# Post-norm transformer layer with routed experts: who makes the low halves and the final sums behind the block loop, and at which tile the last batch's router steps stand

## The reference

```python
def reference(x, w_qkv, w_out, gate_w, gate_b, w1, b1, ..., ws3, bs3):
    x = layernorm(x + attention(x, w_qkv, w_out))         # 16 heads of 16, causal
    # feed-forward: 16 experts of width 176, 6 per token, and a shared one of width 352
    probs = softmax(x @ gate_w.T)
    _, idx = top_k(probs + gate_b, 6)
    for e in range(16):                                   # c is 0 where e was not chosen
        h = silu(x @ W1[e].T + B1[e]) * (x @ W3[e].T + B3[e])
        y += c[e] * (h @ W2[e].T + B2[e])
    z = (silu(x @ ws1.T + bs1) * (x @ ws3.T + bs3)) @ ws2.T + bs2
    return layernorm(x + y + z)
```

## Time and profile before

| what | us |
|---|---|
| three runs of the kernel | 1127.47, 1139.32, 1139.49 (median 1139.32) |
| the profiled execution, its own time | 1130.5 |
| its span, first to last instruction | 1128.7 |
| PE busy in it | 1036.1 (92%) |
| DVE, ACT, POOL busy | 748.7, 670.9, 740.6 |
| mean granted TensorE clock | 0.974 |

### The profile page before, as it was taken

How to read it: one execution, slowest core, us unless ns; L and a number is a source line. 1 busy time by engine, 2 the same in 40 slices (tenths; PEclk the granted TensorE clock), 3 DMA queues, 4 the chain that set the end, 5 groups by cost and what they waited for, 6 DMA issues and landing times.

```text
span 1128.7 us, 28318 instructions
## 1 busy us (share of the span) xinstructions
PE 1036.1 (92%) x8028; PEld 847.3 (75%) x8029; DVE 748.7 (66%) x2401; ACT 670.9 (59%) x1680; POOL 740.6 (66%) x676
## 2 busy tenths in 40 slices
PE   7899998989898998788998999999999999999991
PEld 4546464646464644387988999999999999999991
DVE  8786878786878787577765555555555555555455
ACT  3567676767676765665555555555555555555544
POOL 4224368787878888877635666666666666666665
PEclk9999999999999998899998999999999999999996
DMA  6624254545454535557867666677776666667593
GB/s 185 183 71 114 77 143 147 164 147 163 148 161 145 169 124 172 189 174 228 287 165 139 115 120 119 114 118 117 119 118 113 110 116 113 116 116 140 82 313 144
DMA packets 127037, 163.54 MB, mean 145 GB/s; under 512 B 18800, under 2 KB 107504, under 8 KB 126704
## 3 DMA queue, kind: packets, MB, share of 16 engines
q1 hardware_dynamic: 82240, 99.73, 31.6%
q0 software_dynamic: 39024, 54.29, 25.6%
q10 hardware_dynamic: 5696, 8.55, 2.4%
HBM read 65.36 MB, written 73.85 MB: 123 GB/s over the span
## 4 chain that ended last, share of the span: by engine, by line
PE 63%; DMA 12%; DVE 12%; issue 5%; ACT 4%; POOL 2%; SPq 1%; ACTq 0%; POOLq 0%; DVEq 0%
PE psum L1057 13%; PE psum L794 10%; PE psum L1084 10%; DMA z_d<-y_sb,tokens 9%; PE psum L836 5%; PE psum L824 4%; PE psum L809 4%; DVE rowmax L1496 3%; PE psum L1042 3%; PE psum L1068 3%; PE psum L1053 3%; PE psum L1023 2%; ACT probs L1160 2%; DMA stack_q<-shift_l 2%; PE psum L811 2%
## 5 line engine op out<-in xcount | busy, mean ns | idle before, releaser
L1160 ACT ACTIVATE probs<-psum 128x512 f32<-128x512 f32 (+2 forms) x384 | 186.5, 530 | 115.1 <-PE psum L824 113.2
L1496 DVE TENSOR_REDUCE rowmax<-psum 128x1 f32<-128x512 f32 (+3 forms) x352 | 211.7, 632 | 60.5 <-PE psum L811 58.7
L2029 POOL DMA_INDIRECT xs_d<-x1p,index x192 | 206.1, 1074 | 53.2 <-issue 40.3
L2103 POOL DMA_INDIRECT x_d<-y_sb,tokens x104 | 162.5, 1562 | 93.6 <-ACT y_sb L1354 65.7
L2103 POOL DMA_INDIRECT z_d<-y_sb,tokens x103 | 160.7, 1560 | 93.7 <-ACT y_sb L1354 51.1
L1835 DVE TENSOR_TENSOR xb_lo<-psum,xb_hi 128x256 fp32r<-128x256 f32 x207 | 87.7, 424 | 201.3 <-ACT xb_hi L1151 199.4
L1057 PE MATMUL psum<-we_hi_lo,xb_hi 128*128 x828 | 200.9, 324 | 0.0
L1354 ACT ACTIVATE y_sb<-psum,combine 128x256 f32<-128x256 f32 x207 | 98.3, 475 | 152.2 <-PE psum L1084 75.2
L1084 PE MATMUL psum<-we_hi_lo,hb_hi 88*128 (+1 forms) x828 | 175.2, 304 | 0.0
L809 PE MATMUL psum<-stack_k,stack_q 96*128 96x256 bf16 (+3 forms) x512 | 139.0, 311 | 9.2 <-DVE rowmax L1496 3.6
L1057 PEld LDWEIGHTS psum<-we_hi_lo,xb_hi 128*128 128x128 f32 x828 | 146.8, 190 | 0.0
(11 more groups left out here) (209 smaller groups left out, 2322.3 us busy)
## 6 DMA issues: line engine op xcount, KB each, us to landing
xb<-xs_d SPq DMA_DIRECT2D x207, 138.0 KB
stack_q<-q_h SPq DMA_DIRECT2D x48, 128.0 KB
stack_k<-k_h SPq DMA_DIRECT2D x45, 128.0 KB
w_raw<-in_we SPq DMA_DIRECT2D x9, 608.0 KB, 4.2
xT_raw<-in_xT SPq DMA_DIRECT2D x9, 512.0 KB, 4.2
stack_q<-q_m SPq DMA_DIRECT2D x32, 128.0 KB
stack_k<-k_m SPq DMA_DIRECT2D x32, 128.0 KB
x_res<-in_x SPq DMA_DIRECT2D x8, 512.0 KB, 3.7
```

The lines of the kernel that those rows point to most:

```text
L1160: nc.scalar.activation(probs[kt][:, heads[0]:heads[0] + n, :], st[f % ST_BANKS][:, 0:n * width].rearrange("p (h t) -> p h t", h=n), ACT.Ex ...
L1496: nc.vector.reduce_max(rowmax[gpar][:, heads[0]:heads[0] + n, qt], src, AX.X).then_inc(sm_free, 1)
L2029: nc.gpsimd.indirect_dma_start(out=xs_d[:, :], out_offset=bass.IndirectOffsetOnAxis(ap=index[tp][:, n:n + 1], axis=0), in_=x1p[tp][:, n // ...
L2103: nc.gpsimd.indirect_dma_start(out=(x1_d, z_d)[k % 2][:, :], out_offset=bass.IndirectOffsetOnAxis(ap=tokens[:, k:k + 1], axis=0), in_=y_sb ...
```

## The change

It has two parts.

**Behind the loop.** VectorE makes the low half of every tile to the last, GpSimd none. GpSimd sums `fin_x` and `fin_z` of all 16 units; it runs three units ahead of VectorE's statistics instead of two, and makes no low halves between. The units' statistics begin at tile 38 instead of 39. For units 10 to 15 VectorE adds the PSUM result in one step. ScalarE's `normalized` steps stand one tile earlier with them.

**Ahead of the loop.** The last batch's transposes stand at tile 7 (were 6), its router logits at 9 (8), softmax and choice at 10 (9), the store of its rows at 9 (8), its ranks at 12 (10), the table steps at 13, 14 and 16 (11, 12 and 14).

The rest (`bank_of`, `sum_of` with `SUM_BANKS`, `FINAL_ORDER` as plain order, the counts on `z_stored`) gives the same banks, order and counts as before: 16 units never reach the added wait `hc >= HC1 + SUM_BANKS`. TensorE has the same instructions; VectorE's list is five rows longer and GpSimd's fifteen rows shorter as printed with repeats merged.

```diff
-EPILOGUE_AT = {2: ("t0", "t1"), 4: ("p0", "p1"), 6: ("x0", "x1"), 8: ("r",), 10: ("d",)}
-NORMALIZE_TILE, SOFTMAX_TILE, STORE_X1_TILE, RANK_TILE = 5, 9, 8, 10
+EPILOGUE_AT = {2: ("t0", "t1"), 4: ("p0", "p1"), 7: ("x0", "x1"), 9: ("r",), 12: ("d",)}
+NORMALIZE_TILE, SOFTMAX_TILE, STORE_X1_TILE, RANK_TILE = 5, 10, 9, 12
...
-TABLE_TILES = (11, 12, 14)
+TABLE_TILES = (13, 14, 16)
...
-FINAL_FROM = DVE_LOW_UP_TO = T1 + 9
-SUMS_BY_POOL, NORMALIZED_BY_ACT = HC1 + 2, T_ALL // HT_TOK - 4
+FINAL_FROM, SUMS_AHEAD = T1 + 8, 3
+NORMALIZED_BY_ACT = T_ALL // HT_TOK - 4
+FINAL_ORDER = tuple(range(T_ALL // HT_TOK))
...
         @block.vector
-            def final_add(i):
+            def final_add(m):
 
+                i = FINAL_ORDER[m]
                 dve.wait_ge(down_done, ST * (i + 1))
-                y = sum_of(i).rearrange("p (q d) -> p q d", q=HALF)
-                if i < SUMS_BY_POOL:
-                    dve.wait_ge(fin_sum, i + 1)
-                    nc.vector.tensor_tensor(fin_x[i][:], y, fin_x[i][:], ALU.add).then_inc(z_done, 1)
-                else:
-                    dve.wait_ge(fin_loaded[i], 32)
-                    nc.vector.tensor_tensor(fin_z[i][:], y, fin_z[i][:], ALU.add).then_inc(fin_y, 1)
+                dve.wait_ge(fin_sum, m + 1)
+                nc.vector.tensor_tensor(fin_x[i][:], sum_of(i).rearrange("p (q d) -> p q d", q=HALF), fin_x[i][:],
+                                        ALU.add).then_inc(z_done, 1)
...
             for T in range(T1 + 2, FINAL_FROM + HALVES):
                 if T < T_SH:
                     hide(T)
-                if T - 1 < DVE_LOW_UP_TO:
+                if T - 1 < T_SH:
                     low(T - 1)
...
         @block.gpsimd
-            for T in range(DVE_LOW_UP_TO, FINAL_FROM + HALVES):
-                i = T - FINAL_FROM
-                if i == 0:
-                    final_sum(0)
-                    final_sum(1)
-                if T < T_SH:
-                    low(T)
+            for m in range(SUMS_AHEAD):
+                final_sum(m)
+            for m in range(HALVES):
                 for k, (_, end) in enumerate(FINAL_GROUPS):
-                    if i == end:
+                    if m == end:
                         final_inverse(k)
-                if i + 2 < SUMS_BY_POOL:
-                    final_sum(i + 2)
+                if m + SUMS_AHEAD < HALVES:
+                    final_sum(m + SUMS_AHEAD)
             final_inverse(len(FINAL_GROUPS) - 1)
```

More of the change, by code:

```diff
@@ L516, in postln_layer @@
         TABLE_STEPS = 11
+        SUM_BANKS = 6
         RANKED = 3
@@ L769, in _ @@
                 sp.wait_ge(added[n], 16 * ((BLOCKS + 1 - n) // 2))
-                for i in range(FINAL_FIRST):
+                for i in FINAL_ORDER[:FINAL_FIRST]:
                     load_final(i, src, dst)
-            for i in range(FINAL_FIRST, HALVES):
+            for i in FINAL_ORDER[FINAL_FIRST:]:
                 load_final(i, x1_d, fin_x)
                 load_final(i, z_d, fin_z)
-            for i in range(HALVES):
-                store_final(i)
+            for m in range(HALVES):
+                store_final(m)
             sp.wait_ge(out_stored, 16 * HALVES)
@@ L1020, in shared_down @@
                     pe.wait_ge(z_done, hc - 1)
+                elif t == 0 and hc >= HC1 + SUM_BANKS:
+                    pe.wait_ge(z_done, hc - SUM_BANKS + 1)
                 for j in range(HALF):
@@ L1390, in blocks, with normalized @@
                         split_late_w(m, half)
-            def normalized(i):
-                act.wait_ge(fin_shift_done, [first <= i for first, _ in FINAL_GROUPS].count(True))
-                for q in range(HALF if i < NORMALIZED_BY_ACT else 1):
+            def normalized(m):
+                i = FINAL_ORDER[m]
+                act.wait_ge(fin_shift_done, [first <= m for first, _ in FINAL_GROUPS].count(True))
+                for q in range(HALF if m < NORMALIZED_BY_ACT else 1):
                     last = nc.scalar.activation(fin_x[i][:, q, :], fin_x[i][:, q, :], ACT.Identity,
-                                                bias=fin_shift[:, i, q:q + 1], scale=fin_rstd[:, i, q:q + 1])
+                                                bias=fin_shift[:, m, q:q + 1], scale=fin_rstd[:, m, q:q + 1])
                 last.then_inc(fin_done, 1)
@@ L1465, in _ @@
             high(T_SH - 1)
-            for i in range(T_SH - FINAL_FROM - NORMALIZED_BEHIND, HALVES):
-                normalized(i)
+            for m in range(T_SH - FINAL_FROM - NORMALIZED_BEHIND, HALVES):
+                normalized(m)
         @block.vector
@@ L1900, in final_stats, with final_aggregate, normalized_half @@
                 else:
-                    dve.wait_ge(fin_sum, i + 1)
+                    dve.wait_ge(fin_sum, m + 1)
                 for q in range(HALF):
-                    last = nc.vector.bn_stats(fin_stats[:, i, q, :], fin_x[i][:, q, :])
+                    last = nc.vector.bn_stats(fin_stats[:, m, q, :], fin_x[i][:, q, :])
                 last.then_inc(fin_stats_done, 1)
-            def normalized_half(i):
-                dve.wait_ge(fin_shift_done, [first <= i for first, _ in FINAL_GROUPS].count(True))
-                nc.vector.tensor_scalar(fin_x[i][:, 1, :], fin_x[i][:, 1, :], fin_rstd[:, i, 1:2], fin_shift[:, i, 1:2],
+            def final_aggregate(m):
+                dve.wait_ge(fin_stats_done, m + 1)
+                settle(dve, passed_dve)
+                for q in range(HALF):
+                    last = nc.vector.bn_aggr(fin_mv[:, m, q, :], fin_stats[:, m, q, :])
+                last.then_inc(fin_mv_done, 1)
+            def normalized_half(m):
+                i = FINAL_ORDER[m]
+                dve.wait_ge(fin_shift_done, [first <= m for first, _ in FINAL_GROUPS].count(True))
+                nc.vector.tensor_scalar(fin_x[i][:, 1, :], fin_x[i][:, 1, :], fin_rstd[:, m, 1:2], fin_shift[:, m, 1:2],
                                         ALU.mult, ALU.add).then_inc(fin_half_done, 1)
@@ L1951, in _ @@
                     low_x1(split_x1_of(T))
-                i = T - FINAL_FROM
-                if i >= HC1:
-                    final_add(i)
-                if i >= 1:
-                    final_aggregate(i - 1)
-                if i >= 0:
-                    final_stats(i)
+                m = T - FINAL_FROM
+                if m >= 0 and FINAL_ORDER[m] >= HC1:
+                    final_add(m)
+                if m >= 1:
+                    final_aggregate(m - 1)
+                if m >= 0:
+                    final_stats(m)
             final_aggregate(HALVES - 1)
-            for i in range(NORMALIZED_BY_ACT, HALVES):
-                normalized_half(i)
+            for m in range(NORMALIZED_BY_ACT, HALVES):
+                normalized_half(m)
         @block.gpsimd
```

46 lines of the change are left out of this document (17 added, 29 removed).

## The result

| what | before | changed |
|---|---|---|
| median of 20 runs each, us | 1134.45 (1126.17 to 1140.36) | 1123.29 (1117.81 to 1130.17) |
| ratio, 95% interval | | 0.9908 (0.9889 to 0.9928) |
| the profiled execution's own time | 1130.5 | 1117.81 |
| its span | 1128.7 | 1115.7 |

A forecast was written before the change was run, and what follows sets the result against it. TensorE bounds the loop; only its 10.5 us idle ahead and the 22.2 us after it ends were winnable. 8.7 behind plus 2.5 ahead make 11.2; 1134.9 (middle of four executions) - 11.2 = 1123.7 us, range 1112 to 1134.

The forecast's parts named there:

- the tail: Behind the loop: low halves moved to VectorE and sums to GpSimd were to give 8.7 us, bounds 2.9 and 10.4.
- the front: Ahead of the loop: the reordered last-batch steps were to give 2.5 us by tile 18, bounds nothing and 6.8.
- the low half is never late: Behind the loop: VectorE's turn of 1.6 to 2.2 us against TensorE's 2.19 us tile removes TensorE's 2.09 us wait.
- the rule that I had weighed and not used: Tail: two-SBUF-input VectorE work and GpSimd SBUF reads block fully, up to a whole 1.26 us sum; 0.2 was kept.
- The wait for sum 15: End of the tail: unit 15's sum stands behind the inverse of units 8 to 11; VectorE loses 1.3 us.
- Rival 1: Tail: nine low halves block behind sums, 5.8 us on TensorE, leaving 2.9 of 8.7; 1125.1 us; chance 0.12.
- The waits of 1.5 and 1.7: Ahead of the loop: new TensorE waits for low halves of tiles 9 and 10, about 1.5 and 1.7 us.
- the 0.8 at the transposes: Ahead of the loop, tile 7: down product waits 0.8 us for tile 5's low half; 1.53 goes, gain 0.6.
- The slow tile: Ahead of the loop: tile at TensorE's lower clock, 2.85 instead of 1.60 us, was to go, giving 1.25.
- I take them as caught up just before the loop: Loop entry: the last batch's 24 scatters, starting 3.2 us later, at 1.35 us each, cost nothing.
- Rival 4: Front: scatters become its end, 20 us late at the slow ones' pace; 1139.7 us; chance 0.03.
- rival 2: Front only moves its waits and gives nothing, the tail still 8.7; 1121.8, or 1126.2 at median level; chance 0.22.

The follow-up runs named there:

- experiment 10: Changed kernel with the units behind the loop one tile later (T1 + 9), on a slower chip; first up product behind the loop to span end 64.0 us.
- experiment 2: Kernel before with only the front's new tile numbers, everything behind the loop as before; ratio 0.9993 to before.
- experiment 7: Changed kernel with GpSimd's sums four units ahead instead of three; first up product behind the loop to span end 60.6 us.
- experiment 8: Changed kernel with GpSimd's sums cut to 8 of 512 columns; first up product behind the loop to span end 58.2 us.
- experiment 5: Changed kernel again, no edit; ratio 0.9923 to before, 1123.98 against 1133.34 us.
- experiment 4: Changed kernel with ranks at tile 11 instead of 12 and tables one tile earlier; ratio 0.9949 to before.
- experiment 6: Changed kernel with ranks at tile 11, tables one tile earlier, and the last weight split behind tile 26 instead of 24; ratio 0.9930, 1123.79 us.
- experiment 9: Changed kernel with ranks at tile 14, tables at 15, 16 and 18, on a slower chip (before: 1157.35); 1165.63 us.
- experiment 11: Changed kernel with ranks at 11, last weight split behind tile 26 and sums four units ahead, on a slower chip; ratio 0.9917 to before.
- experiment 12: Changed kernel with units one tile earlier still, sums four ahead, on a slower chip; first up product behind the loop to span end 61.1 us.

## Why the prediction came out

**The total.** The time (1123.7 for 1123.29) and the range held, and the parts behind them less well. By the stretch the tail gives 68.2 (mean of 67.7, 68.1, 68.7) less 61.0 (mean of six traces, 60.1 to 61.5) = 7.2 us for 8.7. By the first block's result (changed front 576.84, 577.90, 577.51, 578.04, 577.15; old front 576.68, 579.10, 578.26) the front gives 0.5 us for 2.5, which by the spread of these could be nothing. That is 7.7 of the 11.2 measured. The other 3.5 us stand in neither part; the loop, which I had put at nothing, is the stage that is left for them. So the agreement of the total to 0.4 us is luck: the tail was put 1.5 us too high, the front 2.0 too high, and 3.5 us that no step of mine has made up for both. What was not luck is the level: the middle of four executions, 1134.9, was the median of before within 0.5 us.

**The tail: mechanism right, 1.5 us too much.**
- TensorE's waits for GpSimd went, as predicted. That "the low half is never late" failed, since I kept the 0.2 us of the earlier trace rows as the price of a sum beside it. Measured excesses are 0.88, 0.29, 0.71 and 0.95 on four low halves and 1.09 on one of x1, 3.9 us in sum.
- This is the rule that I had weighed and not used (the Trainium skill, SBUF — State Buffer, "Who interferes with whom"): the trace agrees with it, two SBUF operands on VectorE against a GpSimd instruction in SBUF, with a block of up to 1.09 us of a sum's 1.26. The rows of before agreed with it too, and I misread them. The first sum and a low half of x1 there, taken alone:

```profile
1080.08 1.30 POOL L2113 TENSOR_TENSOR fin_x<-fin_x,fin_z 128x512 f32<-128x512 f32 x1 [5.84 <-DMA fin_x<-x_d]
...
1092.32 0.77 DVE L1489 TENSOR_TENSOR x1T<-x1T_late,x1T 128x512 fp32r<-128x512 f32 x1 [0.38 <-ACT x1T L1151]
```

The low half of 0.63 us in the earlier trace rows started at 1081.03, late in a sum that ended at 1081.38, and ended 0.28 us behind it: its 0.2 was not the price of a block but the short rest of the sum that it met. And the sum of 1.74 in the earlier trace rows started at 1092.50, inside the 0.77 us above, and ended 1.15 us behind their end at 1093.09, which is nearly a whole sum of 1.26: there it was GpSimd that stood.

- With the blocks the last low half is done 43.5 us into the stretch (1098.48 - 1054.96) where I had 41.3. TensorE ends 1.0 us earlier, not 3.4.
- The wait for sum 15 is 0.72, not 1.3, and gives 0.6 of it back: the last shift moved 7.0 us nearer, with 8 to 9 predicted. The six units at 1.39, the two short inverses and the 5.4 us at the end came out as worked out.
- Rival 1 had the right mechanism with too high a price: a whole sum on each of nine low halves, 5.8 us on TensorE; five instructions were hit by more than 0.1 us, and the changed kernel's stretch is 60.7 us where my steps gave 59.0 (1120.0 - 1061.0). The price is the rest of a sum, and only where one runs.
- Of the 7.2 us, 3 to 4 hang on the units' one tile (experiment 10, one trace) and the rest on the exchange of low halves and sums.

**The front: right until tile 18, wrong at the loop's entry.** The waits of 1.5 and 1.7 came as 1.36 and 1.76, the 0.8 at the transposes as 0.72, and tiles 17 and 18 stand 2.1 and 2.4 us earlier, with 2.2 and 2.5 predicted. The slow tile did not go: the lower clock followed the two new waits as it had followed the one old one. The step that failed is "I take them as caught up just before the loop". I had their start right (525.3, measured 525.9) and their pace nearly (1.35 us each, measured 1.40), had them end at 557.8 where they ended at 559.1, and did not add the landing of the last (3.8 us) and the load of the first rows behind it (2.6 us). 558.1 + 1.0 + 3.8 + 2.6 = 565.5: here TensorE can't start the loop sooner, however early it comes. The scatters had caught up with before (their last ended at 560.1 there), but not with a TensorE that comes 2.1 us earlier: in before, with a landing of 2.0 us and a load of 2.3, their path had no more than 1.3 us of room, in which SP waited for VectorE's low half of x1. In four of the five traces with the ranks at tile 12 (the changed kernel, experiments 2, 7 and 8) the load goes out within 0.2 us of the last landing, and the loop is entered at 565.5 to 566.5; in experiment 5 the late weights hold the entry at the same place. So two things end the front within a microsecond or two of each other, and the landing alone varied from 1.7 to 4.6 us between traces. Rival 4's path (the scatters end the front) was the true one at a price of 2 us instead of 20, and rival 2's time (1126.2) was the better reading of the front. Experiments 2, 4 and 6 show it: with the scatters earlier the wait goes, and with the last split later too the gain gets through to the first block.

**The loop.** What I had not looked for is that the loop has two paces, whatever the kernel: its last 84 blocks take 201 to 203 us in nine traces (among them all three with the old tail) and 195 to 197 in five (the changed kernel's first, and experiments 8, 9, 11 and 12). ScalarE's waits between 862 and 1060 us (total us, times, longest) part them: those for the adding DMAs come to 67 to 76 us over the 84 blocks in each of the nine and to 3.5 to 11 in each of the five. Before:

```profile
ACT y_sb L1354 <- DMA z_d<-y_sb,tokens: 39.9, 41, 2.0
ACT y_sb L1354 <- DMA x_d<-y_sb,tokens: 31.5, 34, 1.3
```

and the changed kernel:

```profile
ACT y_sb L1358 <- PE psum L1088: 43.7, 76, 0.6
...
ACT y_sb L1358 <- DMA x_d<-y_sb,tokens: 5.9, 4, 1.9
```

In the slow pace the copies wait for buffers that the adding DMAs still hold; in the fast one TensorE is the bound. The 5.5 us or so between the paces are nearly half of a kernel's spread of 12 us. Whether the change makes the fast one more frequent (five of eleven traces with the changed tail, none of three without) or only met it in the profiled execution stays open; three of the five are of the slower chip, where four traces were taken. With it stays open what the 3.5 us between 7.7 and 11.2 are, and whether they come again: 7.7 us would be a ratio of 0.9932, just outside the first interval and inside that of experiment 5, and the two parts apart came to 0.9941 together.

## What to carry to other kernels

A wait that is removed pays only up to the next thing that ends there: write down for the place where the stage ends when each of its sources can be ready at the earliest (here scatters, landing, load), not only when the engine can. When work moves between VectorE and GpSimd, count the operands in SBUF: a VectorE instruction with two operands there costs what is left of the GpSimd sum that it meets, up to the whole, and one that reads PSUM costs nothing. A price read off one overlapping pair is a sample of that rest: look at where in the other instruction it started. And where a program's runs spread by 1%, take a second profile of the same kernel before a difference inside an untouched loop is explained.
